# Attention batches written out without a loop, interleaved first steps, an early first gather, and a last tile with buffers of its own

## The reference, cut to what matters

```python
def _L0_xattn_ref(teacher_logits, teacher_features, Wq, bq, Wk, bk):
    query = jnp.einsum('bnc,dc->bnd', teacher_features, Wq) + bq
    key = jnp.einsum('bnc,dc->bnd', teacher_features, Wk) + bk
    energy = jnp.einsum('bnd,bmd->bnm', query, key)
    attention = jax.nn.softmax(energy, axis=-1)
    return jnp.einsum('bln,bmn->blm', teacher_logits, attention)
# x: 4 x 1024 x 1024, context: 4 x 1024 x 512, query/key width 128
x = x + _L0_xattn_ref(_layernorm(x), ctx_1024, ...)
# 4096 rows, 32 experts, the best 4 of a row, inner width 512
h = _layernorm(x)
top, idx = top_k(h @ gate_w.T + gate_b, 4);  weight = softmax(top)
for each of the 4 experts e of a row:
    gate = min(h @ w_gate[e] + b_gate[e], 7);  up = clip(h @ w_up[e] + b_up[e], -7, 7)
    out += weight * (((up + 1) * gate * sigmoid(1.702 * gate)) @ w_down[e] + b_down[e])
x = x + out
```

## Time and profile before

| | |
|---|---|
| median of 3 runs (lowest, highest) | 3232.22 us (3228.62 to 3232.39) |
| profiled execution, time / span | 3231.47 us / 3229.7 us |
| PE, DVE, ACT, POOL busy, share of the span | 96%, 53%, 40%, 18% |
| mean granted clock of PE | 0.979 of full speed |

### The profile page before, as it was taken

The page is one execution under the profiler, slowest core; times in us unless marked ns, Lnnn a source line. Parts: engine busy times, 40 slices in busy tenths (PEclk is TensorE's granted clock), DMA queues, the critical chain, the costliest instruction groups (busy, mean ns, idle before and its releaser), DMA issues.

```text
span 3229.7 us, 46840 instructions
## 1 busy us (share of the span) xinstructions
PE 3088.9 (96%) x15456; PEld 1612.5 (50%) x15457; DVE 1719.9 (53%) x2851; ACT 1294.6 (40%) x1299; POOL 594.1 (18%) x502
## 2 busy tenths in 40 slices
PE   6799899995999999999999999999999999999997
PEld 3465555553444554545545455454554455544553
DVE  3577777774453544554544545554455445554432
ACT  3453444422342433443443434443343434443421
POOL 0023333332111111111111111111111111111111
PEclk8899999997999999999999999999999999999998
DMA  4133323253564555656555657565566555565433
GB/s 152 65 113 124 106 99 107 95 187 125 155 170 110 156 150 156 196 165 192 150 156 151 184 153 206 163 192 142 151 180 173 172 156 150 155 173 133 117 59 59
DMA packets 210439, 468.03 MB, mean 145 GB/s; under 512 B 57761, under 2 KB 57761, under 8 KB 210114
## 3 DMA queue, kind: packets, MB, share of 16 engines
q0 software_dynamic: 45856, 152.33, 21.4%
q10 hardware_dynamic: 94576, 225.46, 20.9%
q1 hardware_dynamic: 69938, 89.38, 8.5%
HBM read 354.64 MB, written 112.46 MB: 145 GB/s over the span
## 4 chain that ended last, share of the span: by engine, by line
PE 75%; DMA 1%; issue 0%; ACT 0%; DVE 0%; SPq 0%; POOL 0%; POOLq 0%
PE psG L1245 23%; PE psU L1245 23%; PE psY L1267 23%; PE psX L1251 4%; PE psA L1258 2%; DMA acc<-y,idxs 0%; DMA idxs<-slots 0%; DMA xg<-xn_tab,idxg 0%; DMA idxg<-slots 0%; DVE y L1192 0%; ACT y L1126 0%; ACT xT L1115 0%; SPq L1041 0%; POOL acc L1083 0%; SPq L1042 0%
## 5 line engine op out<-in xcount | busy, mean ns | idle before, releaser
L1245 PE MATMUL psG<-W,xT 128*128 128x512 f16 x3456 | 771.7, 380 | 2.9 <-ACT xT L1115 2.9
L1267 PE MATMUL psY<-W,aT 128*128 128x512 f16 x3456 | 769.4, 379 | 1.5 <-ACT aT L1119 1.5
L1245 PE MATMUL psU<-W,xT 128*128 128x512 f16 x3456 | 769.4, 379 | 0.0
L1245 PEld LDWEIGHTS psG<-W,xT 128*128 128x128 f16 x3456 | 338.5, 98 | 412.6 <-issue 5.2
L1267 PEld LDWEIGHTS psY<-W,aT 128*128 128x128 f16 x3456 | 338.1, 98 | 377.2 <-ACT aT L1119 1.7
L1245 PEld LDWEIGHTS psU<-W,xT 128*128 128x128 f16 x3456 | 338.2, 98 | 375.6
L123 DVE SCALAR_TENSOR_TENSOR W<-stage,W 128x2048 f16<-128x2048 f32 x192 | 438.7, 2285 | 3.8 <-ACT W L118 3.8
L1192 DVE SCALAR_TENSOR_TENSOR y<-bias,idxs,y 128x1024 f32<-128x1024 f32 x144 | 185.0, 1285 | 460.3 <-ACT y L1126 460.3
L1083 POOL DMA_INDIRECT acc<-y,idxs x144 | 226.3, 1571 | 990.4 <-DVE y L1192 974.9
L118 ACT ACTIVATE W<-stage 128x2048 f16<-128x2048 f32 x192 | 365.8, 1905 | 48.5 <-issue 37.9
L650 PE MATMUL psM<-W,XT 128*128 (+1 forms) x1392 | 369.9, 384 | 10.8 <-issue 9.1
(11 more groups left out here) (140 smaller groups left out, 2372.5 us busy)
## 6 DMA issues: line engine op xcount, KB each, us to landing
stage<-in_L_ffn_w_down ACTq DMA_DIRECT2D x62, 1024.0 KB, 6.6
stage<-in_L_ffn_w_up ACTq DMA_DIRECT2D x61, 1024.0 KB, 7.2
stage<-in_L_ffn_w_gate ACTq DMA_DIRECT2D x60, 1024.0 KB, 8.3
stage<-in_x SPq DMA_DIRECT2D x32, 512.0 KB, 4.8
xr<-in_x SPq DMA_DIRECT2D x32, 512.0 KB, 4.4
acc<-xr SPq DMA_DIRECT2D x32, 512.0 KB, 3.1
xn_tab<-x2h SPq DMA_DIRECT2D x32, 512.0 KB, 3.0
bias<-in_L_ffn_b_down ACTq DMA_DIRECT2D x32, 512.0 KB
```

Source lines behind the costliest of these rows:

```text
L1245: op = pe.matmul(ps[:], xT[:, k, :, a], weights(par, c, offset + k * I, I), start=k == 0 and n == 0, stop=k == KH - 1 and n == 2)
L1267: op = pe.matmul(psY[:, h * HALF:(h + 1) * HALF], aT[:, k, :, a], weights(par, c, 2 * KH * I + k * H + h * HALF, HALF), start=k == 0 and n ...
```

## The change

1. `schedule` runs the three iterations of the batch loop as Python, so the code is written out three times with constant batch numbers; `more` is then a Python truth value, and `guarded` either emits the part or leaves it out. No hardware loop or `If` is left in the overlapped batches.
2. A new helper `beside_product` says which steps take the path of `both`: besides s >= 2 also s = 1 of the first overlapped pair and s = 0 and 1 of the later pairs that prepare a next batch. ACT takes its order of such steps there too; at s = 0 it evacuates the probabilities of tile 7 first.
3. In `both`, the row transposes move from matmuls 6 to 13 of the first half to matmuls 10 to 17, the logits from 0 to 7 to 2 to 9 of the second half.
4. The transposes of the probabilities of tile 7 move into `queries_and_keys`, between its first and second quarter, behind waits for `s_xTev` and `s_alo`; only the last batch keeps them at step 0.
5. At the end of the first block SP waits for the stored rows and for all slot scatters, loads the first tile's slots into `idxg`, and POOL waits for that and issues the first gather; both buffers and their semaphores now outlive the block. The second block starts without its first load and gather.
6. The last expert tile has `idxs_last` and `y_last`: its slots are loaded right after those of the tile before, and ACT no longer waits for `s_added` there. Its scatter still waits for the one before.

```diff
 def guarded(eng, cond, body):
-    if cond is None:
+    if cond is None or cond is True:
         body()
-    else:
+    elif cond is not False:
         with eng.If(cond):
             body()
...
-            with eng.Fori(0, B - 1) as b:
+            for b in range(B - 1):
...
+        def beside_product(s, b1, b2, more):
+            return b1 is not None and b2 is not None and lagged(b2, s, 1) is not None and (s >= 2 or more is not False)
...
@@ sync, end of the first block
             for t in range(2):
+                sp.wait_ge(s_xnout[t], 16 * (B * NT // 2 + 1))
+            for t in range(2):
+                sp.wait_ge(s_slotout[t], 16 * TOPK * (B * NT // 2))
+            sp.dma_start(g["idxg"][:], slots[0:P, :]).then_inc(g["s_idxg"], 16)
+            for t in range(2):
                 sp.wait_ge(s_x2out[t], 16 * B * NT // 2)
-            for t in range(2):
-                sp.wait_ge(s_xnout[t], 16 * (B * NT // 2 + 1))
@@ gpsimd, end of the first block
-            for t in range(2):
-                pool.wait_ge(s_slotout[t], 16 * TOPK * (B * NT // 2))
+            pool.wait_ge(g["s_idxg"], 16)
+            pool.indirect_dma_start(out=g["xg"][:], out_offset=None, in_=xn_tab[:, :],
+                                    in_offset=bass.IndirectOffsetOnAxis(g["idxg"][:, 0:1].bitcast(U32), 0)).then_inc(g["s_xg"], 16)
@@ scalar, step
-                if s >= 2 and b1 is not None and b2 is not None:
+                if beside_product(s, b1, b2, more):
                     bt, n = late
+                    if s == 0:
+                        attention_out(b2, NT - 1)
                     exponent()
...
-                    attention_out(b1, s - 1)
+                    if s > 0:
+                        attention_out(b1, s - 1)
@@ tensor, queries_and_keys
                 for n in range(4):
+                    if n == 1 and not first(bk):
+                        pe.wait_ge(s_xTev, NT * batch(bk))
+                        pe.wait_ge(s_alo, NT * batch(bk))
+                        transpose_words(ah_w[(NT - 1) % 2], s_AT)
@@ tensor, both
-                bt, n = b2, s - 1
+                bt, n = lagged(b2, s, 1)
+                held = range(10, 10 + KH)
                 def x2_beside(m):
-                    if m == 6:
-                        alone(pe, s_xTev, tile(b1, s), s_past)
+                    if m == held[0]:
+                        if s == 0:
+                            pe.wait_ge(s_ATev, tile(b2, NT))
+                        else:
+                            pe.wait_ge(s_xTev, tile(b1, s))
                         pe.wait_ge(s_xs2, tile(bt, n + 1))
-                    if 6 <= m < 6 + KH:
-                        transpose_block(xs2, s_x2T, m - 6)
+                    if m in held:
+                        transpose_block(xs2, s_x2T, m - held[0])
                 def logits_beside(m):
-                    if m == 0:
+                    if m == 2:
                         pe.wait_ge(s_x2Tev, tile(bt, n + 1))
...
-                    if m < KH:
-                        logits_block(m)
+                    if 2 <= m < 2 + KH:
+                        logits_block(m - 2)
                 def probs_beside(m):
+                    if s == 0:
+                        return
...
+                if s == 0:
+                    pe.wait_ge(s_ATev, tile(b2, NT))
                 product(psM, b2, s, 0, range(KH), x2_beside)
...
-                pe.wait_ge(s_ATev, tile(b1, s))
+                if s > 0:
+                    pe.wait_ge(s_ATev, tile(b1, s))
+                else:
+                    pe.wait_ge(s_x2Tev, tile(bt, n + 1))
@@ tensor, step
-                if b2 is not None and s == 0:
+                if b2 is not None and s == 0 and batch(b2) == B - 1:
@@ vector, step
-                    if n < 2 and not isinstance(bt[0], int):
-                        with dve.If(bt[0] > 0):
-                            alone(dve, s_slotout[j], per(8 * NT * TOPK, bt, 0), s_past)
-                    else:
+                    if n >= 2 or batch(bt) > 0:
                         dve.wait_ge(s_slotout[j], per(8 * NT * TOPK, bt, 16 * TOPK * (n // 2)))
@@ experts
-            load_slots(sp, idxg, 0, s_idxg)
...
             tt = start_of(sp, E)
-            alone(sp, s_added, tt, s_past)
-            load_slots(sp, idxs, tt - 1, s_idxs)
+            load_slots(sp, idxs_last, tt - 1, s_idxl)
...
-            gather(0)
...
-            scatter(tt - 1)
+            alone(pool, s_y, tt, s_past)
+            pool.indirect_dma_start(out=acc[:, :], out_offset=bass.IndirectOffsetOnAxis(idxs_last[:, 0:1].bitcast(U32), 0),
+                                    in_=y_last[:], in_offset=None, compute_op=ALU.add).then_inc(s_scat, 16)
...
-            weigh_y(tt - 1)
+            act.wait_ge(s_idxl, 16)
+            act.wait_ge(s_Y, tt)
+            act.activation(y_last[:], psY[:], ACT.Copy, scale=idxs_last[:, 2:3].bitcast(F32)).then_inc(s_y0, 1)
...
-            finish_y(tt - 1, 1)
+            dve.wait_ge(s_y0, tt + 1)
+            dve.scalar_tensor_tensor(out=y_last[:], in0=bias[:, 1, 2 * I:], scalar=idxs_last[:, 1:2].bitcast(F32), in1=y_last[:],
+                                     op0=ALU.mult, op1=ALU.add).then_inc(s_y, 1)
```

More of the change, by code:

```diff
@@ L103, in xattn_moe_kernel @@
         s_wlo = whole.enter_context(nc.semaphore("weights_lo"))
+        idxg = whole.enter_context(nc.sbuf_tensor("idxg", [P, 4], I32))
+        xg = whole.enter_context(nc.sbuf_tensor("xg", [P, 2 * H], F16))
+        s_idxg = whole.enter_context(nc.semaphore("gather_idx_in"))
+        s_xg = whole.enter_context(nc.semaphore("rows_gathered"))
         w_dram = [w.rearrange("e (k p) n -> e p k n", p=P) for w in (w_gate, w_up, w_down)]
@@ L983, in experts @@
         bias = sb("bias", [P, 2, 2 * I + H], F32)
-        idxg = sb("idxg", [P, 4], I32)
+        idxg, xg, s_idxg, s_xg = g["idxg"], g["xg"], g["s_idxg"], g["s_xg"]
         idxs = sb("idxs", [P, 4], I32)
-        xg = sb("xg", [P, 2 * H], F16)
+        idxs_last = sb("idxs_last", [P, 4], I32)
         xT = sb("xT", [P, KH, P, 2], F16)
```

7 lines of the change are left out of this document (4 added, 3 removed).

## The result

The changed kernel takes 3196.64 us (median of 4 runs, 3193.78 to 3198.88) against 3230.8 us for the kernel before, measured beside it: a ratio of 0.9894, 95% interval 0.9877 to 0.9911, or 34.2 us less. Run again beside most of the experiments it took 3195.31 us (3194.77 to 3195.93) against 3232.96, ratio 0.9886 (0.9869 to 0.9902), 37.6 less. The profiled executions stand at spans of 3229.7 and 3192.9 us, 36.8 apart, so 11.2 us have to be explained.

What follows compares the result with a forecast made beforehand. Experts bound by PE alone; gains lie in the overlapped batches (PE paces context steps, DVE the others), the block boundary and the end. 11.3 + 2.2 + 2.4 + 4.6 + 5.1 = 25.6 us less: 3206.5 us, range 3198 to 3216.

Steps and rivals of the forecast that it cites:

- DVE's floor of 18.0: In overlapped steps without context DVE needs about 18.0 us and sets the pace, so PE's idle time there is slack: 0.
- Loop return: Writing out the batch loop removes PE's two jumps back, which lengthened two steps by 6.3 and 5.0 us: 11.3 us less.
- PE was late and nobody else: In the two steps with a loop return, DVE's residual sum waited 3.74 and 2.32 us for PE, so only PE was late.
- Rivals B: Half the loop gain returns as code-fetch stalls, or the clock drops at all three ends of step 7: 3212 to 3215; 0.12.
- D: Straight code is not kept ahead of PE, issue gaps of 2.3 us each: slower, 3261 with one per overlapped step; chance 0.03.
- Steps 0 and 1: Interleaved order in overlapped batches: 0.9 us less in two steps 1, 0.45 in the first, 0 at step 0; 2.2 together.
- Clock: PE's granted clock after its wait at the end of step 7, three places: 0, between -3 and +3 us.
- Positions: Later row transposes and logits cover PE's 0.30 us wait in each of eight context steps: 2.4 us less; other steps 0.
- Probability transposes: Eight transposes, 0.9 us of PE, moved into queries and keys; their waits are covered and step 0 gives the time back: 0.
- First gather: At the block boundary, slot load and first gather issued before the barrier start PE's experts 4.6 us earlier (2.5 to 5.3).
- the case that the prediction called uncovered: At the block boundary, POOL's drain waits until the gathered rows have landed; PE would start near 769.8, hardly worse.
- Last tile: Own buffers let ACT start right after the last product instead of behind the previous scatter: 5.1 us less (4.9 to 5.3).

Runs made afterwards that it cites:

- e2: The kernel before with its batch loop written out on TensorE (PE) alone, the other engines keeping the loop: 3224.01 us, 8.0 less.
- e14: e8 plus filler matmuls on PE, whose results nothing reads, at the logits of step 1 (four) and the end of step 7 (eight): 3199.05 us.
- e8: The changed kernel with steps 0 and 1 written plainly again and a batch's last probability transposes back in its step 0: 3205.08 us, 9.8 slower.
- e9: The kernel before with eight filler matmuls on PE, whose results nothing reads, behind the product of step 7: 3227.46 us, 5.4 less.
- e10: The changed kernel with eight filler matmuls on PE, whose results nothing reads, in the idle time at the end of step 7: 3193.60 us.
- e7: The changed kernel with the row transposes back at matmul 6 and the logits back at 0: 3200.21 us, 4.9 slower.
- e12: The changed kernel with SP's last 1 MB weight load issued behind the first gather and DVE's last weight cut held until the slots landed: 3192.34 us.
- e6: The changed kernel with the last tile's index and output buffers shared again: 3203.54 us, 8.2 slower.

## Why the prediction was off, step by step

In the profiled span the sum was short by 11.2 us. 4.6 of them are clock (1.8 in one step 0, 2.8 in the last), where its term said 0 within 3. 3.4 are steps 0 and 1, which won 5.6 without that clock where the term said 2.2. 2.1 are the plain steps, for which DVE's floor of 18.0 said 0. The other parts together make about 1.

*Loop return, -11.3:* held. 11.5 us by the loop written out alone, 12.1 in the changed kernel. The step "PE was late and nobody else" was wrong (e2), without a price here. Rivals B and D are refuted: PE has no issue wait between 140 and 620 us, and in the changed kernel's two profiles the clock fell at none of the three ends of step 7. The Trainium skill (Runtime: NRT & Kernel Launch, Instruction fetch mechanics) has sequential code fetched ahead, and a taken branch to code outside the fetched window as a stall; the traces fit both, with 3.6 and 4.0 us at the branch back and no issue wait in straight code. That the branch waited for code, and not for something else, no run shows.

*Steps 0 and 1, -2.2:* the largest term that was mis-sized. Without the clock they won 5.6 us from profile to profile: 4.5 by the order (e14 against the changed kernel, by the trace), and 1.1 since these steps became 0.2 to 0.3 us shorter even in the plain order (18.83 before, 18.56 in e14), as the plain steps did. Two sizes were wrong. The first step 1 was set at the middle of 0 and 0.9 and was 1.8. It has fewer instructions on DVE (29, busy 13.5 us, instead of 47 and 15.1, since there is no tile two back yet), and so could fall to 16.5 us, under the 17.9 taken as its end. Step 0 was set at 0, by letting the moved transposes eat all that DVE won; the order gave 0.5 each. Besides, PE's waits were costed by their length alone: where the clock falls behind a wait of 0.9 us in step 1, it costs another 1.6 (e8, e14).

*Clock, 0 within -3 to +3:* the step that failed. The prediction argued from the length of PE's wait at the end of step 7, and since that would not shrink, it put the clock at nothing. The wait did not shrink (1.92 and 1.96 us), yet 4.6 us of clock were won. In the profile of the kernel before the clock fell at two of its three places, worth 1.8 and 2.8 us; filling the gap there gave 5.4 us (e9: 3225.93 to 3229.02, the kernel before beside it 3229.36 to 3233.94). In the changed kernel's first two profiles it fell at none, and e10 gives 1.7. The price was too low as well: the prediction took 1.2 us a place from one stretch of queries and keys, and did not read the third place, the last step 0, which took 20.27 us at a granted clock of 0.83. That the clock does not follow from the wait alone, 5 falls in 24 equal places show. Why 2 us of idle time tip it more often in the old order (8 of 15) stays open. Fewer and shorter waits ahead of it (4.9 us for `xs2` instead of 10.2, no plain step) would fit, but no run varied them by themselves. That the clock came out well in the profiled executions is in part luck: the upper two of the first four runs (3198.5 and 3198.9) lie inside the forecast's range.

*Positions, -2.4:* the mechanism held (context steps shorter, plain ones unchanged in e7). Seven ordinary context steps became 0.42 us shorter each, not 0.30. PE's wait of 0.30 went whole; the 0.1 beyond it is not explained. In the changed kernel the new positions are worth 0.55 a step and something in four steps 0 and 1 that the sum left out (e7: 4.9 us), since without them the wait would be 0.56.

*"DVE's 18.0 is its floor":* wrong. 18.03 was one row; the nine plain steps of the kernel before took 17.70 to 18.12, on average 17.86. L918 showed no wait for PE in them, and still they became 0.23 us shorter each, 2.1 us in nine, since DVE's own work did: 0.13 went with DVE's loop, 0.10 with the addresses of its buffers. The sum had no term for either. The prediction listed this floor as what it would fail by.

*Probability transposes, 0:* not separated from step 0; together with its order they won 0.5 us in each of two steps 0.

*First gather, -4.6:* held, by the case that the prediction called uncovered. 4.1 by the median and 4.3 by the trace. The drain waits for the gathered rows, PE starts 0.1 us behind the barrier, and the price of that case (769.8 instead of 769.4, so 4.2 us won) is what came. What it took as fixed was not: the slots landed 7.7 us after the start of the last scatter (7.4 before), and without the weight load and the cut beside it they land after 2.2 (e12).

*Last tile, -5.1:* 5.4 to 5.5 from the last product to the end, in e6 and between the two profiles. The step held.

The sum of the single terms measured one by one against the changed kernel (9.8 + 4.9 + 4.1 + 8.2) and of the loop (15.9) is 42.9, more than the 37.6 of the whole: several of these runs carry the same falls of the clock.

## What to carry to other kernels

A wait of TensorE costs its own length and, where the granted clock falls behind it, more: here 1.6 us behind a wait of 0.9, and 1.7 to 2.8 behind one of 1.9. Look at the clock in each step of the profile, before and after, and try whether a few matmuls into a free PSUM bank in the gap bring it back. A step whose last operation shows no wait is not at a floor: look at what its instructions are made of. A step's length is to be read over all its repetitions, not from one row (18.03, where nine gave 17.86).

## Of the hardware, not expected

- Moving buffers by 4112 bytes a partition made two DVE operations of 1024 columns 50 ns shorter (1429 to 1379, 1353 to 1304), and a POOL scatter beside them 1.3 us shorter (2.98 to 1.67).
- The drain ahead of a block's barrier on POOL waits for an outstanding gather: 5088 ns, 5597 in e12, 1367 with none.
- The loop returns of other engines hide behind that of PE: with PE's gone, DVE's and ACT's showed 2.2 and 2.6 us (e2).
- Whether 2 us of idle TensorE time lowers the clock differs from execution to execution of one kernel, and one of them is worth 1.7 to 2.8 us.
